# Inverse roots of the norms as powers of minus one half on GpSimd, in a two-layer attention and mixture-of-experts kernel

## The reference

```python
x = x + _layernorm(attn(_layernorm(x)))      # block one
x = x + _layernorm(ffn(_layernorm(x)))       # block two

# block one: xn = x * rsqrt(mean(x*x) + EPS) * g1; Q, K, V; elu of Q and K
kv1 = einsum('bshe,bshd->bsed', K1, V) * SCALE      # kv2 from K2
attn = w1 - lmb * w2                                # w1 = Q1 kv1, w2 = Q2 kv2
attn = (1 - LAMBDA_INIT) * _rms(attn, g2)           # over the 16 numbers of a head
attn = _rms(attn, g3) + attn                        # over the 256 of a row
out = gelu(attn @ W1.T) @ W2.T + attn

# block two: rms norm, causal attention with 16 heads of 16 and rotary positions,
# rms norm, router with the top 2 of 8 experts, silu(g) * u, down projection
```

## Time and profile before

| what | value |
|---|---|
| median of 3 runs | 4219.42 us |
| the profiled execution: its time | 4222.84 us |
| its span, first to last instruction | 4221.0 us |
| PE busy | 3289.6 us (78%) |
| DVE busy | 2406.3 us (57%) |
| ACT busy | 1688.5 us (40%) |
| POOL busy | 1416.1 us (34%) |
| mean granted TensorE clock | 0.897 of full speed |

### The profile page before, as it was taken

How to read it: one execution, slowest core, us unless ns; L and a number is a source line. 1 busy time by engine, 2 the same in 40 slices (tenths; PEclk the granted TensorE clock), 3 DMA queues, 4 the chain that set the end, 5 groups by cost and what they waited for, 6 DMA issues and landing times. The chain is left out here.

```text
span 4221.0 us, 54252 instructions
## 1 busy us (share of the span) xinstructions
PE 3289.6 (78%) x17636; PEld 1957.6 (46%) x17637; DVE 2406.3 (57%) x4542; ACT 1688.5 (40%) x3774; POOL 1416.1 (34%) x1041
## 2 busy tenths in 40 slices
PE   6788668776878696769677966886788499999991
PEld 4444544354336333533453354435444266666660
DVE  5875577476838672967386558755775222222226
ACT  2456245525541554256335623562456122222223
POOL 7510840093019202820462055206510222222222
PEclk9899889888988898889888989897899699999996
DMA  1000000000000000000000000000000533333335
GB/s 54 10 11 11 21 20 2 15 18 20 2 31 2 21 2 31 0 21 2 31 0 21 2 31 11 11 1 31 10 1 11 172 59 55 55 60 55 56 52 165
DMA packets 85955, 125.48 MB, mean 30 GB/s; under 512 B 11600, under 2 KB 70864, under 8 KB 83664
## 3 DMA queue, kind: packets, MB, share of 16 engines
q1 hardware_dynamic: 59216, 85.40, 6.5%
q0 software_dynamic: 26496, 37.01, 5.0%
HBM read 58.23 MB, written 63.36 MB: 29 GB/s over the span
## 5 line engine op out<-in xcount | busy, mean ns | idle before, releaser
L699 ACT ACTIVATE PR<-SP_ 128x512 f32<-128x512 f32 (+3 forms) x1536 | 693.8, 489 | 457.8 <-PE SP_ L1285 311.0
L976 DVE TENSOR_REDUCE NM<-MX 128x1 f32<-128x128 f32 (+7 forms) x1024 | 732.6, 752 | 230.2 <-PE MX L1254 219.9
L423 POOL DMA_INDIRECT scratch_xs<-FX,SLOT x128 | 123.7, 966 | 1461.0 <-issue 1459.5
L465 POOL TENSOR_TENSOR work<-QK,VS 128x2048 f32<-128x2048 f32 x128 | 519.8, 4084 | 15.7 <-DVE QK L811 15.5
L1282 PE MATMUL SP_<-work,KST 99*128 99x512 bf16 (+3 forms) x1536 | 467.8, 332 | 44.0 <-ACT PR L699 32.1
L1252 PE MATMUL MX<-KST,work 96*128 96x512 bf16 (+3 forms) x1536 | 435.3, 346 | 73.8 <-DVE NM L976 60.4
L1547 POOL DMA_INDIRECT scratch_h<-Y,XG x136 | 210.6, 1549 | 618.9 <-DVE Y L1610 525.0
L1588 DVE TENSOR_TENSOR AG<-UB,SL 128x512 f32<-128x512 f32 x136 | 94.0, 691 | 477.8 <-PE UB L1627 477.8
L1157 PE MATMUL OB<-work,ident 128*128 128x256 f32 x1024 | 269.4, 429 | 77.7 <-POOL work L465 77.7
L1298 PE MATMUL OA<-PR,V 128*32 128x512 f32 (+3 forms) x3072 | 327.3, 498 | 3.3 <-ACT PR L699 3.3
L865 DVE TENSOR_REDUCE AT<-work 128x208 f32<-128x3328 f32 x56 | 324.6, 5796 | 0.0
(11 more groups left out here) (256 smaller groups left out, 5435.7 us busy)
## 6 DMA issues: line engine op xcount, KB each, us to landing
XG<-scratch_xs SPq DMA_DIRECT2D x136, 130.0 KB, 2.1
X<-in_L_attn_x SPq DMA_DIRECT2D x8, 1024.0 KB, 5.6
scratch_x<-X SPq DMA_DIRECT2D x8, 1024.0 KB, 3.9
scratch_h<-A SPq DMA_DIRECT2D x8, 1024.0 KB, 3.9
X<-scratch_x SPq DMA_DIRECT2D x16, 512.0 KB, 4.0
HH<-scratch_h SPq DMA_DIRECT2D x16, 512.0 KB, 4.5
out<-X SPq DMA_DIRECT2D x16, 512.0 KB, 3.1
wg<-in_L_ffn_Wg SPq DMA_DIRECT2D x1, 4096.0 KB, 17.3
```

The source lines that it names most:

```text
L465: sg["prod1"].by(pool.tensor_tensor(P1[t % 2][:, i * hh * D:(i + 1) * hh * D].rearrange("p (h e d) -> p h e d", h=hh, e=HD), QK[:, t % 3, ...
L699: sg["exp"].by(act.activation(PR[:, n % 8, q0:512], SP_[:, n % 2, q0:512], ACT.Exp))
L976: sg["mx"].by(dve.tensor_reduce(NM[:, qt, h:h + 1], src, AX.X, ALU.max, negate=True))
```

## The change

All square roots of ACT inside the batches, and the one of the setup, go. The reciprocals of DVE behind them go too. In their place POOL raises the same numbers to the power of -0.5, in one `tensor_tensor` with a tile `minus_half` that the setup fills. DVE or ACT then waits for POOL. Where two factors are needed (`uC`), POOL makes both in one instruction of 8 numbers and DVE multiplies twice instead of once. The table of the root is used only in `finish`.

```diff
+        minus_half = sb("minus_half", [P, CH * H])
...
+            ps_.by(pool.memset(minus_half[:, :], -0.5))
...
+            def inverse_root(done, out, x, ready, k):
+
+                pool.wait_ge(ready.sem, k)
+                n = 1
+                for d in x.shape[1:]:
+                    n *= d
+                power = minus_half[:, 0:n]
+                if len(x.shape) == 3:
+                    power = power.rearrange("p (a b) -> p a b", b=x.shape[2])
+                done.by(pool.tensor_tensor(out, x, power, ALU.pow))
+
+            inverse_root(setup["root"], st[:, 10, :], st[:, 9, :], setup["u"], 2)
...
+                    if t == NT:
+                        inverse_root(sg["rt16"], R16[:, chunk_slice(0)], R16[:, chunk_slice(0)], sg["m16"], 1)
                     if t >= 3:
                         gain2(t - 3)
+                    if t == NT + 1:
+                        inverse_root(sg["rrow"], st[:, 6, chunk_slice(0)], st[:, 5, chunk_slice(0)], sg["m1"], 1)
+                inverse_root(sg["rt16"], R16[:, chunk_slice(1)], R16[:, chunk_slice(1)], sg["m16"], 2)
+                inverse_root(sg["rrow"], st[:, 6, chunk_slice(1)], st[:, 5, chunk_slice(1)], sg["m1"], 2)
                 sg["ag"].settle(pool)
+                for c in range(NCH):
+                    x = chunk_slice(c)
+                    inverse_root(sg["rt2"], st[:, 3, x], st[:, 0, x], sg["uB"], c + 1)
+                    inverse_root(sg["rt2"], st[:, 2:4, x], st[:, 0:2, x], sg["uC"], c + 1)
...
+                for c in range(NCH):
+                    x = chunk_slice(c)
+                    inverse_root(sg["rt2"], st[:, 8, x], st[:, 8, x], sg["u3"], c + 1)
+                inverse_root(sg["rt2"], st[:, 10, :], st[:, 9, :], sg["u1"], 2)
                 end_batch(pool, "pool")
...
-                root(sg["rt16"], R16[:, chunk_slice(1)], sg["m16"], 2)
                 attention_turned(0)
                 squared_rows(1)
-                root(sg["rtrow"], st[:, 5, chunk_slice(1)], sg["m1"], 2)
                 gains(1)
                 hidden(0)
                 attention_turned(1)
-                root(sg["rt2"], st[:, 0, chunk_slice(0)], sg["uB"], 1)
                 layer_normed(0)
                 hidden(1)
-                root(sg["rt2"], st[:, 0:2, chunk_slice(0)], sg["uC"], 1)
...
                     dve.wait_ge(sg["rt2"].sem, root_of)
-                    ds.by(dve.reciprocal(st[:, 3, x], st[:, 0, x]))
                     if second:
-                        ds.by(dve.reciprocal(st[:, 2, x], st[:, 1, x]))
-                    ds.settle(dve)
-                    if second:
-                        ds.by(dve.tensor_tensor(st[:, 2, x], st[:, 2, x], st[:, 0, x], ALU.mult))
+                        ds.by(dve.tensor_tensor(st[:, 2, x], st[:, 2, x], st[:, 3, x], ALU.mult))
+                        ds.settle(dve)
+                        ds.by(dve.tensor_tensor(st[:, 2, x], st[:, 2, x], st[:, 1, x], ALU.mult))
                         ds.settle(dve)
```

More of the change, by code:

```diff
@@ L205, in attention_kernel @@
         h2d = dram["h2"][0:B * S].rearrange("(p g) f -> p g f", p=P)
-        POOL_SETUP = 11 + 12
+        POOL_SETUP = 11 + 12 + 1
         NWLOAD = 5 + 3 + 1 + 1 + 2 + 3 + 1 + 1
@@ L520, in _ @@
             setup["act"].by(act.activation(lam[:, 6:8], lam[:, 4:6], ACT.Exp))
-            act.wait_ge(setup["u"].sem, 2)
-            setup["root"].by(act.activation(st[:, 9, :], st[:, 9, :], ACT.Sqrt))
-            act.wait_ge(setup["coef"].sem, 2)
+            act.wait_ge(setup["coef"].sem, 1)
             with act.Fori(0, B) as b:
@@ L560, in squares @@
                     sg["sq"].by(act.activation(SQ[:, u % 2], AT[:, u], ACT.Square))
-                def root(done, x, ready, k):
-                    act.wait_ge(ready.sem, k)
-                    done.by(act.activation(x, x, ACT.Sqrt))
                 def squared_rows(c):
@@ L618, in _ @@
                         kv_sums(t - 1)
-                    if t == NT:
-                        root(sg["rt16"], R16[:, chunk_slice(0)], sg["m16"], 1)
                     if t == NT + 1:
@@ L626, in _ @@
                     if t == NT + 1:
-                        root(sg["rtrow"], st[:, 5, chunk_slice(0)], sg["m1"], 1)
                         gains(0)
-                root(sg["rt16"], R16[:, chunk_slice(1)], sg["m16"], 2)
                 attention_turned(0)
                 squared_rows(1)
-                root(sg["rtrow"], st[:, 5, chunk_slice(1)], sg["m1"], 2)
                 gains(1)
@@ L656, in _ @@
                 turned(0)
-                root(sg["rt2"], st[:, 0, chunk_slice(1)], sg["uB"], 2)
                 layer_normed(1)
@@ L661, in _ @@
                         turned(t + 1)
-                    if t == 0:
-                        root(sg["rt2"], st[:, 0:2, chunk_slice(1)], sg["uC"], 2)
                     if t < NT:
@@ L716, in _ @@
                         squares2(t - 2)
-                    if t == CH + 2:
-                        root(sg["rt2"], st[:, 8, chunk_slice(0)], sg["u3"], 1)
                 squares2(NT - 2)
                 squares2(NT - 1)
-                root(sg["rt2"], st[:, 8, chunk_slice(1)], sg["u3"], 2)
                 for t in range(NT):
@@ L726, in _ @@
                     sg["fT"].by(act.activation(XN[:, t % 2], SP_[:, t % 2, 0:D], ACT.Copy))
-                root(sg["rt2"], st[:, 9, :], sg["u1"], 2)
                 act.wait_ge(sg["lgs"].sem, 1)
@@ L794, in x_coefficients @@
                 dve.wait_ge(rooted.sem, k)
-                done.by(dve.reciprocal(st[:, 10, :], st[:, 9, :]))
-                done.settle(dve)
                 done.by(dve.scalar_tensor_tensor(out=st[:, 11, :], in0=mv[:, :, 0], scalar=-1.0, in1=st[:, 10, :],
@@ L820, in norm_heads @@
                     dve.wait_ge(sg["rt16"].sem, c + 1)
-                    sg["r16"].by(dve.reciprocal(R16[:, chunk_slice(c)], R16[:, chunk_slice(c)]))
-                    sg["r16"].settle(dve)
                     dve.wait_ge(sg["ag"].sem, CH * (c + 1))
@@ L832, in scale_row_squares @@
                     sg["m1"].by(dve.tensor_scalar(x, x, 1.0 / D, EPS1, ALU.mult, ALU.add))
-                def invert_rows(c):
-                    dve.wait_ge(sg["rtrow"].sem, c + 1)
-                    sg["rrow"].by(dve.reciprocal(st[:, 6, chunk_slice(c)], st[:, 5, chunk_slice(c)]))
                 def add_gains(c):
@@ L931, in add_residual @@
                     sg["stats2"].settle(dve)
-                    ds.by(dve.tensor_scalar(st[:, 0, x], mv[:, x, 1], LN_EPS, None, ALU.add))
+                    ds.by(dve.tensor_scalar(st[:, 1, x], mv[:, x, 1], LN_EPS, None, ALU.add))
                     ds.settle(dve)
-                    sg["uC"].by(dve.scalar_tensor_tensor(out=st[:, 1, x], in0=st[:, 0, x], scalar=LN_EPS, in1=mv[:, x, 1],
+                    sg["uC"].by(dve.scalar_tensor_tensor(out=st[:, 0, x], in0=st[:, 1, x], scalar=LN_EPS, in1=mv[:, x, 1],
                                                          op0=ALU.mult, op1=ALU.add))
@@ L1031, in flatten @@
                     dve.wait_ge(sg["rt2"].sem, 5 + c)
-                    ds.by(dve.reciprocal(st[:, 8, x], st[:, 8, x]))
-                    ds.settle(dve)
                     sg["h2"].settle(dve)
```

2 lines of the change are left out of this document (removed).

## The result

The kernel before ran at 4220.52 us (median of six, 4217.84 to 4226.72), the changed kernel at 4437.99 us (median of six, 4435.79 to 4440.5). The ratio is 1.0514 with a 95% interval of 1.05 to 1.0527. Forecast were 4203.4 us and a range from 4180 to 4290. What came is the rival that had been given 0.12, the very dear power.

What follows compares the result with a forecast made beforehand. It took block one's norms as bound by a chain of small operations, hand-overs and table loads; terms sum to -2.44 us a batch, -19.5 in eight, +3.5 once, total -16.0: 4203.4 us, range 4180 to 4290.

Steps and rivals of the forecast that it cites:

- the very dear power: Rival: a power costs over 80 ns a number, up to 1150; 4290 us and beyond; chance 0.12.
- The unknown price: A power of n numbers on POOL takes 0.19 us plus 17 ns a number, counted as eight passes.
- the slope: Each further 1 ns a number costs 0.172 us a batch, 1.4 us in all; no change at 28.5 ns.
- Part 1: First half of the heads: DVE's scaling starts later behind a power of 64 numbers, +1.17 us a batch.
- Parts 2 and 3: First-half rows' norm -0.03 us a batch; second half to gelu +0.19, the later of DVE's and PE's paths deciding.
- Parts 4 and 5: First-half uB through HS, then second half up to POOL's rotation: together -2.81 us a batch, from saved table loads and waits.
- Part 6: Router: -0.33 for the first half, -0.03 for the second, -0.60 from u1 to the logits, us a batch.
- The setup: Once: the setup's power stands on POOL ahead of 16 scattering DMAs and delays them, +3.5 us.
- The gain hidden anyway: Rival: the rotation stage has its pace from elsewhere, so the gain is hidden; counted within break-even, chance 0.18.

Runs made afterwards that it cites:

- e1_mult: The changed kernel with every power replaced by a product with 1.0, so the inverse roots are left out; 4218.94 us, 0.9996 of before.
- e2_r16_back: The changed kernel with only the two 64-number roots of R16 a batch put back on ACT and DVE; 4274.64 us, 1.0126 of before.
- h4_after_warm12: The changed kernel plus unused matmuls in PE's waits, 4 and 12 at the start of a batch; 4414.66 us, 1.046 of before.
- e4_uB0: The kernel before with only the first half's uB root as a power of 4 numbers on POOL; 4218.24 us, 0.9992 of before.
- g2_uB0_warm: The kernel before with the first half's uB power on POOL and unused matmuls in PE's waits (6 and 24 at batch start); 4210.6 us, 0.9975.
- h1_warm12: The kernel before plus unused matmuls in PE's waits, 4 and 12 at the start of a batch; 4211.8 us, 0.9977 of before.
- h2_uB0_warm12: The kernel before with the first half's uB power on POOL and unused matmuls (4 and 12 at batch start); 4186.44 us, 0.9917.
- g3_mult_warm: The changed kernel with products by one for powers and unused matmuls in PE's waits (6 and 24 at batch start); 4186.63 us, 0.992 of before.
- g1_warm: The kernel before plus unused matmuls in PE's waits, 6 and 24 at the start of a batch; 4237.42 us, 1.0035 of before.
- e3_r16_only: The kernel before with only the two inverse roots of R16 a batch moved to POOL as powers; 4410.53 us, 1.0449 of before.

## Why the prediction was wrong, step by step

**The unknown price** is the step that failed. It took 0.19 + 0.017 us a number, eight passes of a product; the power takes 0.37 + 0.159. The error is one of size, ninefold, and the slope that the prediction gave decides the rest. A batch has 2 powers of 64, 6 of 4 and 3 of 8 numbers: 2 x 10.56 + 6 x 1.01 + 3 x 1.64 = 32.1 us, where the prediction had 2 x 1.28 + 6 x 0.26 + 3 x 0.33 = 5.1. The difference, 27.0 us, is 216 in eight batches. With it the prediction's own sum, -19.5 for the parts and now +2.75 for the setup, gives +199 us. Measured were +217.5. So for its large term the chain sum is about right. That it comes so near is in part luck: the 19.5 us of forecast gains did not arrive (e1_mult, whose chain gives still more, is 1.5 us under the kernel before), and the 2.2 us a batch that PE loses at its lower level behind the long stops were in no term. The rival was priced ("4290 and beyond") but had a chance of 0.12. Its upper bound, a software job at 1150 ns, was seven times too high. The nearest row, a product at 2.1 ns, was 76 times too low, and the eight passes that the prediction made of it nine times.

**Part 1**: +1.17 forecast. DVE waits 10.84 us for the first half's power (timeline above). By the same sum with the measured price it is +10.45 (150.65 + 10.56 + 0.03 against 150.79).

**Parts 2 and 3**: the rows' norm went from 0.64 us (156.50 to 157.14) to 1.28 in the first batch (169.33 at L835 to 170.61); forecast was a small gain. The second half's wait for the power is 10.66 us. The PE path that was to decide part 3 no longer does.

**Parts 4 and 5**: `uB` to `layer_normed` went from 2.48 us to 1.55 (199.85 to 201.40); forecast 0.64 from the end of `uB`, measured 1.38. The power of 4 takes 0.75 more than assumed, and that is all the difference. From `uB` to `HS` it is 8.59 us instead of 9.17, a gain of 0.6 where 2.58 were forecast. Gelu's second table load is gone, and it starts with its matmuls at 204.16, as forecast. `uC` to `HS` went from 2.17 to 2.51 us (205.93 to 208.44), a loss instead of a gain. No load stands in it now, but a power of 1.64 us and one product more.

**Part 6** and its -0.96 us: even with products in place of the powers (e1_mult) DVE is early and waits for PE; nothing of it reaches the batch.

**The setup**: +3.5 forecast; the first DMA went from 25.20 to 27.95 us, +2.75. The power was dearer here too, but the variances were ready 2.35 us earlier (L800 at 25.73, where L793 of before stands at 28.08): 28.73 - 2.35 + 1.36 for the power and its hand-over (1.84 instead of 0.48) + 0.21 to the first DMA is 27.95. The earlier time is not the change's: in e1_mult, the same program with a product for each power, L800 stands at 27.93 and the first DMA at 29.16.

**What no term held** is PE's level. The earlier trace rows has its granted clock, 0.89, and the prediction used it nowhere. Two things follow. The long waits put PE at its lower level behind them: between gelu and `HS` the changed kernel takes 2.22 us a batch more than e2_r16_back, some 18 of the 217.5 us. The added matmuls of h4_after_warm12 do not touch these stages, so the 23.3 us that they win on the changed kernel are no measure of that. And the gains of the loads, 4.50 us a batch in e1_mult and 1.55 in e4_uB0, were given back in later stages. In two of them the granted clock was lower than in the kernel before: 0.70 instead of 0.80 ahead of the exponential in e4_uB0, and 0.50 instead of 0.63 ahead of the routing weights in e1_mult. The 1.50 us that e1_mult gives back ahead of the last product come without it: from first to last product the granted clock is 0.89 in it (1266.50 to 1365.99 us) and 0.88 in the kernel before (1266.26 to 1364.25).

**The gain hidden anyway** is the rival that the prediction argued away, since the rotation waits for its releaser. That was right as far as it went: measured from gelu, the rotation of e1_mult starts 3.08 us earlier (22.38 us behind it, and 25.46 before). But the argument stopped at the next hand-over. e1_mult, whose products are cheaper than the power that was forecast, shows 0.9996; so with a power at the forecast price no gain was to be expected either, and not 16 us.

What stays open: why the length of a batch falls on few values. In the fourth batch it is 406.1 to 406.3 us in the kernel before, e1_mult, e4_uB0, g2_uB0_warm and h1_warm12, 402.7 in h2_uB0_warm12 and g3_mult_warm, 409.6 in g1_warm, though their stages differ by up to 4.5 us; with the long stops it is 433.5, and 430.1 in h4_after_warm12. So a saving of 1.55 us a batch showed as nothing in one pair of kernels and as 3.4 in another. The granted clocks of the stretches and the effect of the added matmuls say that PE's level takes part in it. Why it does so nearly exactly was not tried, and no run holds the level fixed, so the give-back itself is argued from these two and not isolated. Nor is it settled why the 190 us of e3_r16_only and the 54 of e2_r16_back exceed the 217.5 of the change by 27.

## What to carry to other kernels

An operation that no row of the trace shows needs a price before anything is moved onto it; here its place in the sum (172 numbers in a chain, eight times) was worth 200 us, and a probe of nine instructions settles it. In these runs a power on GpSimd shortened its own stage only at 4 numbers a partition and where it took table loads out of the chain; without such a load the power of 4 made its stretch longer (0.64 to 1.28 us in part 2). And where the matmul engine waits often, a shorter chain is worth its microseconds only if the clock is looked at in the stages behind it; here one power that gave nothing by itself gave 0.8% together with a few matmuls without use in the waits, and the matmuls alone 0.23%.
